# Attention over edges: TensorE sums a block's second group before, not after, its product for ScalarE's last slot

## What is computed

```
w_m = (efeat @ W_msg + b_msg).reshape(E, 16, 16)
w_a = (efeat @ W_attn + b_attn).reshape(E, 16, 16)
h_src = feat[src][:, :, None]
e1, e2 = w_m * h_src, w_a * h_src
ex = exp(e2 - segment_max(e2, dst)[dst])
attn = ex / segment_sum(ex, dst)[dst]
out = x + segment_sum(e1 * attn, dst).sum(axis=1)
```

## Time and profile before

| what | value |
|---|---|
| median of three runs | 2709.7 us (2708.16 to 2709.81) |
| span of the profiled execution, first to last instruction | 2774.5 us |
| DVE busy over the span | 2233.7 us, 81% |
| PE busy | 2191.1 us, 79% |
| ACT busy | 1763.9 us, 64% |
| POOL busy | 1321.9 us, 48% |
| mean granted TensorE clock, share of full speed | 0.847 |

### The profile page before, as it was taken

The page is one execution under the profiler, slowest core; times in us unless marked ns, Lnnn a source line. Parts: engine busy times, 40 slices in busy tenths (PEclk is TensorE's granted clock), DMA queues, the critical chain, the costliest instruction groups (busy, mean ns, idle before and its releaser), DMA issues. The chain is left out here.

```text
span 2774.5 us, 36642 instructions
## 1 busy us (share of the span) xinstructions
PE 2191.1 (79%) x7895; PEld 960.2 (35%) x7896; DVE 2233.7 (81%) x3857; ACT 1763.9 (64%) x6869; POOL 1321.9 (48%) x1141
## 2 busy tenths in 40 slices
PE   1688888898699984488888888888888888888870
PEld 0344444466455532123222222222222222222220
DVE  7799999314587702399999999999999999999996
ACT  6577777013111111588888888888888888888843
POOL 5000000405550002577767777677777777777704
PEclk9899999888899996588888888888888888888885
DMA  3000000205785431012222222222222222222214
GB/s 69 6 0 0 0 0 0 93 1 177 244 259 179 139 116 23 19 52 71 71 71 71 71 71 71 70 63 71 71 71 71 71 71 71 71 71 71 66 57 123
DMA packets 109221, 205.35 MB, mean 74 GB/s; under 512 B 38652, under 2 KB 66980, under 8 KB 103406
## 3 DMA queue, kind: packets, MB, share of 16 engines
q1 hardware_dynamic: 67278, 156.49, 16.0%
q0 software_dynamic: 41888, 48.19, 8.0%
HBM read 76.22 MB, written 128.34 MB: 74 GB/s over the span
## 5 line engine op out<-in xcount | busy, mean ns | idle before, releaser
L1803 POOL DMA_INDIRECT hs<-h_table,gix x860 | 1081.6, 1258 | 434.5 <-issue 241.8
L1914 ACT ACTIVATE e<-wps,hs 128x32 f32<-128x32 f32 x5632 | 1030.6, 404 | 227.5 <-PE wps L1844 158.9
L1844 PE MATMUL wps<-w_edge,ef 18*128 18x512 f32 x1760 | 578.8, 706 | 301.1 <-ACT e L1914 162.6
L1866 PE MATMUL slot_sums<-e,ident 128*128 128x512 f32 x1392 | 757.0, 694 | 8.5 <-DVE e L2018 7.0
L1866 PEld LDWEIGHTS slot_sums<-e,ident 128*128 128x128 f32 x1392 | 294.8, 223 | 489.0 <-issue 463.7
L1844 PEld LDWEIGHTS wps<-w_edge,ef 18*128 18x128 f32 x1760 | 159.3, 200 | 678.1 <-ACT e L1914 309.8
L526 ACT CAST edges<-acc 128x400 f32 x600 | 295.0, 492 | 102.0 <-PE acc L513 75.3
L509 PE MATMUL acc<-q_hot,lo_hot 128*128 128x400 bf16 x1200 | 307.4, 338 | 53.3 <-DVE q_hot L483 51.4
L1953 DVE TENSOR_TENSOR e<-wps,hs 128x2048 f32<-128x2048 f32 x132 | 301.6, 2285 | 54.9 <-remote 23.0
L551 POOL DMA_INDIRECT got<-in_edge_rows,start x64 | 65.1, 1018 | 543.9 <-POOLq L464 417.6
L483 DVE TENSOR_SCALAR q_hot<-qcol,qT 128x400 bf16<-128x400 bf16 x1200 | 290.5, 317 | 1.0 <-PE acc L513 0.9
(11 more groups left out here) (381 smaller groups left out, 1964.0 us busy)
## 6 DMA issues: line engine op xcount, KB each, us to landing
rows_state<-states SPq DMA_DIRECT2D x43, 1280.0 KB
rows_shift<-shifts SPq DMA_DIRECT2D x44, 640.0 KB
got_order<-edges_order SPq DMA_DIRECT2D x56, 256.0 KB
ef_order<-efT SPq DMA_DIRECT2D x56, 256.0 KB
hs<-h_table,gix POOLq DMA_INDIRECT x880
ef<-ef_order SPq DMA_DIRECT2D x44, 320.0 KB
edges_order<-got POOLq DMA_DIRECT2D x32, 256.0 KB
edges_order<-msg_parts POOLq DMA_DIRECT2D x24, 256.0 KB
```

The costliest lines, as they stand in the source:

```text
L1803: nc.gpsimd.indirect_dma_start(out=hs[u][:, s, :], out_offset=None, in_=d["h_table"], in_offset=bass.IndirectOffsetOnAxis(ap=gix[u][:, s:s ...
L1844: nc.tensor.matmul(wps[:, bank, :], ef[u][k:k + KM, g * P:(g + 1) * P], w[k:k + KM, :], start=True, stop=True).then_inc(a_mult, 1)
L1866: ins = nc.tensor.matmul(sums[:, g % 2, :], ident[:, :], e[u][:, g * SLOTS + c, :], start=(c == 0), stop=(c == SLOTS - 1))
L1914: ins = nc.scalar.mul(e[u][:, s, at], wps[:, bank, at], hs[u][:, s, f:f + 1])
```

## The change

`period` gets a fourth argument, `following`, which is block b-1, the block after `before`. The sum of group 1, which stood first in a block's period, is taken from there, and the same sum of the same block is issued near the end of the period before, between the product for slot 14 and the product for slot 15.

```diff
-                def period(u, b, before):
+                def period(u, b, before, following):
...
-                    add(1)
                     for_act(u, b, (4,))
                     add(0)
...
                     for_dve(u, b, 2, NV + 2)
-                    for_act(u, b, (13, 14, 15))
+                    for_act(u, b, (13, 14))
+                    if following is not None:
+                        summed(1 - u, following, 1)
+                    for_act(u, b, (15,))
...
-                period(0, 0, None)
+                period(0, 0, None, None)
...
-                period(1, 1, None)
+                period(1, 1, None, 0)
...
-                        period(u, i * 2 + (2 + u), i * 2 + u)
-                for g in (1, 0, *range(2, BYPE)):
+                        period(u, i * 2 + (2 + u), i * 2 + u, i * 2 + (u + 1))
+                for g in (0, *range(2, BYPE)):
```

## The result

The changed kernel takes 2858.0 us (median of four runs, 2855.13 to 2860.93) against 2708.9 before: a ratio of 1.0543, with a 95% interval of 1.0531 to 1.0556. It is 149 us slower. The forecast was 2807 with a range up to 2855; the sign is as forecast, and the time lies above the range.

What follows compares the result with a forecast made beforehand. DVE sets the pace, with ACT's slot 15 on the path; a net loss of 2.27 us a block over 43 blocks gives 98 us, added as 97 to the median: 2807 us, range 2755 to 2855.

Steps and rivals of the forecast that it cites:

- Product to ACT: From the start of a product on PE to ACT's first instruction on it: 1.15 us.
- ACT's own gain: ACT's waits for products 4 and 5 (3.07 and 1.73 us) go, but its exponentials still follow DVE's subtractions: worth nothing.
- no slack: At line 1973 DVE meets ACT's end of slot 15 in every block, so any lateness there delays DVE in full.
- blocks A to C: Three blocks in a row of the first profile, with `weigh` beginning at 1887.85, 1922.48 and 1956.82, used to work out the loss.
- How long the sum takes: The moved sum on PE keeps its present length in the same block: 5.19, 4.98 and 6.52 us.
- How late slot 15 is: ACT's slot 15, behind the moved sum and product 15, starts 2.87, 2.49 and 4.20 us later.
- What comes back: Sum 0 comes earlier, so DVE's wait at line 2053 goes: 0.63, 0.16 and 1.97 us.
- Rival 1: The moved sum runs slow throughout, 6.52 us in every block: 139 us lost, 2848 us; chance 9 in 100.
- Rival 2: The moved sum brings PE's clock up and takes 3.63 us: 14 us lost, 2724 us; chance 8 in 100.
- Rival 3: Faster: only DVE's wait at line 2053 goes, slot 15 is not late: 40 us won, 2670 us; 6 in 100.
- rival 4: No difference: idle time elsewhere on DVE takes up the delay; chance 5 in 100.

Runs made afterwards that it cites:

- the second profile: The kernel before, without an edit, profiled once more: 0.9997 of before, with a span of 2709.1 us.
- fill: Identity matmuls added behind products 12 (two), 13 (two) and 14 (one): 2768.7 us in the changed kernel, 2713.9 us in the order of before.

## Why the forecast missed

**The mechanism was right.** The sum starts with the second `weigh` (1880.33 worked out, 1880.46 in the trace). Product to ACT takes 1.15 us forecast, 1.16 measured. Slot 15 is late, DVE pays at `largest` (some 150 us forecast, 162.5 in 41 blocks measured), the wait at line 2053 goes, and ACT's own gain is worth nothing. A block was forecast at about 37.3 us, and takes 37.5.

**The step that failed is the base.** The prediction worked out its loss, 98 us, against the blocks of the profiled execution, and put it (as 97) on top of the median of the runs; of the 64.8 us between the two it said that "nothing on the page says in which stage" they lie. By the second profile 43.0 us lay in the very loop that was costed. In that one execution ACT lost 0.75 us a block to "issue". Its slot 15 came only when DVE was already waiting, product 15 and with it sum 1 came late too, and DVE waited 0.86 us at line 2053 in place of 0.44. A block took 35.04 us; in the second profile it takes 34.04, and ACT has 0.47 us to spare. So "no slack" held for that execution and not for the kernel. The forecast of the changed block was close, and the subtraction started from the wrong block: 37.46 - 34.04 = 3.42 us, times 43 is 147, where 2.27 times 43 was 98.

That the forecast of the changed block holds although its base does not has a reason. There slot 15 waits for `weigh`, the sum and product 15, and what held ACT up before it no longer counts (ACT is idle 4.32 us ahead of slot 15). Some of the closeness is luck: slot 15 starts 9.47 us after the first `weigh` (1887.44 - 1877.97), where the working gives a mean of 9.07, and the rest of the block is shorter than in the first profile. The choice of blocks A to C is not the cause: the same working on 40 blocks of that profile gives 2.25 us a block. And on the second profile it gives a loss of about 3.2 us (slot 15, which starts at 1919.57 there, is late by 1916.94 + 5.78 + 1.15 - 1919.57 = 4.30; less 0.47 of slack, 0.44 at line 2053 and 0.2 at line 1953), 137 us in all and 2846 for the kernel.

**Its terms, against the second profile.** *How long the sum takes*: a mean of 5.56 us in blocks A to C; in the changed kernel it is 5.82 (1880.46 to 1886.28). *How late slot 15 is*: 3.19 us mean forecast, 4.32 of ACT's idle time measured, as an ACT that is not held up gets to slot 15 sooner. Of that, DVE sees 3.96. *What comes back*: 0.92 us forecast at line 2053, 0.45 in the second profile, with 0.2 for the products of line 1953. 3.96 - 0.45 - 0.2 makes 3.3 of the 3.4 us a block.

**The rivals.** Rival 1 named 2848 us, for a sum that is slow throughout; the time came near it, but by accident: the sum was 0.26 us longer than the forecast's mean, and not 0.96. Rival 2, that the moved sum brings the clock up by itself, did not happen, and where fill holds the clock up there is still a loss of some 1.9 us a block. Rival 3 and rival 4 fell with the sign; the gain at line 2053 that rival 3 spoke of is real, 18 us, once it is taken without touching product 15.

**What stays open.** The runs do not show what held ACT up in the first profile of before. The 22.4 us that the loop started later there are for the most part the same hold-up: ACT's first slot of the attention starts only 2.2 us later (1098.78 against 1096.57), and its eighth ends 29.1 us later (1158.54 against 1129.46).

## What to carry to other kernels

An instruction that is moved forward on an engine that works in order is paid for by what it is moved past: ask first when the thing behind it is needed, and by whom (here product 15, needed 2.9 us after product 14, stood behind a sum of 5.8). A profiled execution that is far off the median is a warning about every slack read from it: find the stage in which the difference lies, or profile again, before its waits are costed. And a wait of a consumer may be taken away on the consumer's side, by other work put ahead of it; here this won 0.7%.

## What the runs showed of the hardware

One execution of the same program took 65.4 us longer than another, with 67.2 us of ACT's idle time that no event explains in the one and none in the other. The rhythm of the changed kernel is strikingly even: from the sixth step of `weigh` to the fortieth each block takes 37.54 or 37.55 us, with DVE's wait for ACT at 3.95 or 3.96 us and the clock rising inside the moved sum every time. The first profile of before mostly went through three lengths in turn, 36.0, 35.1 and 34.6 us from `weigh` to `weigh`, with 6.6, 5.7 and 5.2 us for sum 1; blocks A to C lie at one of two places where a block of 34.3 us comes in between the earlier trace rows. In the stretch of the earlier trace rows with the granted clock at 0.50, PE did two thin products (18 of 128 rows at work) and the first rows of a sum, and stood idle 3.0 of 10.2 us; in the changed kernel the clock fell, between 1864.4 and 1884.9, with no idle stretch of PE above 1.31 us. Whether the idle time or the thin products let it fall, no run here separates.
